# Graph layer on one Trainium2 core: the clique rows of the mix as two scaled f16 planes instead of three bf16 planes

## What is computed

```python
gathered = x_clique[clique_idx]                                   # edges x 128
summed = jax.ops.segment_sum(gathered, node_idx, num_segments=n_nodes)
count = jax.ops.segment_sum(jnp.ones(...), node_idx, num_segments=n_nodes)
mean = summed / jnp.maximum(count, 1.0)[:, None]
out = mean @ W.T + b
```

## Time and profile before

| what | value |
|---|---|
| median of 3 runs | 2649.56 us (2644.44 to 2656.32) |
| the profiled execution: its own time | 2649.81 us |
| its span | 2648.0 us |
| mean granted TensorE clock | 0.92 of full |
| PE busy | 2353.2 us, 89% |
| PEld busy | 2075.0 us, 78% |
| DVE busy | 1588.0 us, 60% |
| ACT busy | 1271.9 us, 48% |
| POOL busy | 109.5 us, 4% |

### The profile page before, as it was taken

How to read it: one execution, slowest core, us unless ns; L and a number is a source line. 1 busy time by engine, 2 the same in 40 slices (tenths; PEclk the granted TensorE clock), 3 DMA queues, 4 the chain that set the end, 5 groups by cost and what they waited for, 6 DMA issues and landing times.

```text
span 2648.0 us, 58999 instructions
## 1 busy us (share of the span) xinstructions
PE 2353.2 (89%) x20705; PEld 2075.0 (78%) x20705; DVE 1588.0 (60%) x2721; ACT 1271.9 (48%) x3044; POOL 109.5 (4%) x88
## 2 busy tenths in 40 slices
PE   1479999999999999999987799999998625999897
PEld 1369999999999999999975577777787614888644
DVE  8668777777777777777755555555575483000033
ACT  1246666666666666666611466666786410000133
POOL 3100000000000000000000000000000240000000
PEclk6589999999999999999965899999999857999899
DMA  5401111111111111111143422222384146888321
GB/s 166 123 33 73 73 68 54 73 73 73 49 73 73 73 58 63 73 73 69 52 114 92 173 106 105 105 105 105 138 315 164 48 117 255 300 302 299 98 62 56
DMA packets 183684, 299.35 MB, mean 113 GB/s; under 512 B 13256, under 2 KB 136523, under 8 KB 183523
## 3 DMA queue, kind: packets, MB, share of 16 engines
q1 hardware_dynamic: 179488, 284.33, 30.9%
q0 software_dynamic: 4144, 14.34, 1.9%
HBM read 198.15 MB, written 100.49 MB: 113 GB/s over the span
## 4 chain that ended last, share of the span: by engine, by line
PE 80%; DVE 9%; issue 3%; DVEq 3%; DMA 3%; ACT 1%; POOLq 0%; SPq 0%; POOL 0%; ACTq 0%; PEldq 0%
PE ps L703 21%; PE ps L762 18%; PE ps L692 15%; PE ps L686 8%; PE ps L746 7%; PE ps L801 4%; PE ps L895 2%; PE ps L732 2%; DVE hT_s L1272 1%; DVE carry L1469 1%; DVE big L1198 1%; DMA hs<-node_rows 1%; PE ps L620 1%; PE ps L792 1%; DMA big<-edge_counts 1%
## 5 line engine op out<-in xcount | busy, mean ns | idle before, releaser
L703 PE MATMUL ps<-big,rows_area 128*128 128x128 f32 x4802 | 659.6, 278 | 0.0
L703 PEld LDWEIGHTS ps<-big,rows_area 128*128 128x128 f32 x4802 | 587.6, 191 | 0.1
L1001 ACT CAST edge_area<-ps 128x392 f16<-128x392 f32 x784 | 380.9, 486 | 410.8 <-PE ps L686 410.8
L762 PE MATMUL ps<-big,rows_area 128*128 128x256 f16 (+1 forms) x4900 | 543.6, 272 | 25.9 <-DMA big<-edge_counts 25.9
L692 PE MATMUL ps<-edge_area 128*128 128x196 f16 x4704 | 540.7, 249 | 0.0
L762 PEld LDWEIGHTS ps<-big,rows_area 128*128 128x128 f16 x4900 | 469.6, 98 | 79.4 <-DMA big<-edge_counts 26.1
L692 PEld LDWEIGHTS ps<-edge_area 128*128 128x128 f16 x4704 | 421.4, 97 | 0.3
L1007 ACT COPY big<-ps 128x392 f32<-128x392 f32 x784 | 381.7, 487 | 29.8 <-PE ps L692 1.3
L686 PE MATMUL ps<-edge_area 128*128 128x196 f16 x2352 | 335.1, 250 | 15.2 <-DVEq L1421 15.2
L1416 DVE TENSOR_TENSOR edge_area<-lo_pair,carry 128x768 f16<-128x768 f16 x392 | 218.7, 558 | 211.5 <-PE ps L692 166.3
L1417 DVE TENSOR_TENSOR edge_area<-cell_pair,carry 128x1176 f16<-128x1176 f16 x392 | 299.6, 764 | 0.0
(11 more groups left out here) (210 smaller groups left out, 1650.5 us busy)
## 6 DMA issues: line engine op xcount, KB each, us to landing
big<-edge_counts SPq DMA_DIRECT2D x336, 448.0 KB, 4.9
edge_counts<-edge_area SPq DMA_DIRECT2D x49, 1568.0 KB, 5.7
hs<-node_rows POOLq DMA_DIRECT2D x21, 448.0 KB, 4.5
edge_area<-in_x SPq DMA_DIRECT2D x14, 448.0 KB
x_stream<-edge_area SPq DMA_DIRECT2D x14, 448.0 KB, 4.0
node_rows<-edge_area SPq DMA_DIRECT2D x14, 448.0 KB
edge_area<-x_stream SPq DMA_DIRECT2D x14, 448.0 KB, 3.9
node_rows<-rows_area SPq DMA_DIRECT2D x7, 448.0 KB
```

The source lines that it names most:

```text
L703: last = mm(p_sum[par], h0[:, n, :], w32[:, par, n, :], start=(n == 0), stop=(n == NB - 1))
L762: last = mm(p_block[par][:, 0:width, :], planes[:, p, sh, :], piece[:, par, k, 0:width, j, :], start=(sh == 0 and p == 0), stop=(sh == NB ...
L1001: nc.scalar.copy(store_slot[:, par, :, cols], p_count[s % 2]).then_inc(sem("count_taken"), 1)
```

## The change

The clique rows are no longer split into three bf16 planes. For each clique row VectorE takes the largest absolute value, keeps the exponent of it (a power of two, `xc_unit`), and scales the row by its inverse; the scaled row goes into two f16 planes. The mix then has two planes, 8 matmuls for 12. The power of two is put back on the other side of the product: ScalarE's copy of the flipped counts becomes an activation with a per-partition scale, `xc_unit`, and writes bf16 instead of f16. That copy therefore waits for the split of its own block, once at k = 0 of each block.

```diff
-        xc_plane = take(2 * 2 * 3 * D // 2, BF16).rearrange("p (s c l n) -> p s c l n", s=2, c=2, l=3)
+        xc_plane = take(2 * 2 * 2 * D // 2, F16).rearrange("p (s c l n) -> p s c l n", s=2, c=2, l=2)
         xc_in = take(2 * D)
-        xc_r = take(2 * D)
-        xc_r2 = take(2 * D)
-        flipped = take(4 * W // 2, F16).rearrange("p (s c n) -> p s c n", s=2, c=2)
+        xc_top, xc_inv = take(2), take(2)
+        xc_unit = take(4).rearrange("p (s c) -> p s c", s=2)
+        flipped = take(4 * W // 2, BF16).rearrange("p (s c n) -> p s c n", s=2, c=2)
...
-                            for l in range(3):
+                            for l in range(2):
                                 last = mm(p_mix[:, lo:hi], xc_plane[:, par, c, l, :], flipped[:, odd, c, lo:hi],
-                                          start=(c == 0 and l == 0), stop=(c == 1 and l == 2))
+                                          start=(c == 0 and l == 0), stop=(c == 1 and l == 1))
...
-                def copy_flip(n, c, odd):
+                def copy_flip(n, c, odd, par):
                     act.wait_ge(sem("flips"), n * 2 + c + 1)
                     act.sem_inc(sem("act_passed"), 1)
                     if c == 0:
 
                         act.wait_ge(sem("mixed"), n + 1)
-                    nc.scalar.copy(flipped[:, odd, c, :], p_flip[c]).then_inc(sem("flip_copied"), 1)
+                    nc.scalar.activation(flipped[:, odd, c, :], p_flip[c], ACT.Copy, scale=xc_unit[:, par, c:c + 1]).then_inc(
+                        sem("flip_copied"), 1)
...
                         if cliques:
-                            copy_flip(b * SUBS + k, 0, (par + k) % 2)
-                            copy_flip(b * SUBS + k, 1, (par + k) % 2)
+                            if k == 0:
+                                act.wait_ge(sem("xc_split"), b + 2)
+                                act.sem_inc(sem("act_passed"), 1)
+                            copy_flip(b * SUBS + k, 0, (par + k) % 2, par)
+                            copy_flip(b * SUBS + k, 1, (par + k) % 2, par)
...
-                rows, r, r2 = (v.rearrange("p (c d) -> p c d", c=2) for v in (xc_in, xc_r, xc_r2))
-                plane = [xc_plane[:, par, :, l, :] for l in range(3)]
+                rows = xc_in.rearrange("p (c d) -> p c d", c=2)
+                unit = xc_unit[:, par, :]
                 dve.wait_ge(sem("xc_loaded"), b * 16 + 16)
-                V.tensor_copy(plane[0], rows)
-                dve.drain()
-                V.tensor_tensor(r, rows, plane[0], ALU.subtract)
-                dve.drain()
-                V.tensor_copy(plane[1], r)
-                dve.drain()
-                V.tensor_tensor(r2, r, plane[1], ALU.subtract)
-                dve.drain()
-                V.tensor_copy(plane[2], r2).then_inc(sem("xc_split"), 1)
+                V.tensor_reduce(xc_top, rows, AX_X, ALU.max, apply_absolute_value=True)
+                dve.drain()
+                V.tensor_scalar(xc_top, xc_top, 1e-30, None, ALU.max)
+                dve.drain()
+                V.tensor_scalar(unit.bitcast(I32), xc_top.bitcast(I32), 0x7f800000, None, ALU.bitwise_and)
+                dve.drain()
+                V.reciprocal(xc_inv, unit)
+                dve.drain()
+                for c in range(2):
+                    V.tensor_scalar(xc_plane[:, par, c, 0, :], rows[:, c, :], xc_inv[:, c:c + 1], None, ALU.mult)
+                dve.drain()
+                for c in range(2):
+                    last = V.scalar_tensor_tensor(out=xc_plane[:, par, c, 1, :], in0=rows[:, c, :], scalar=xc_inv[:, c:c + 1],
+                                                  in1=xc_plane[:, par, c, 0, :], op0=ALU.mult, op1=ALU.subtract)
+                last.then_inc(sem("xc_split"), 1)
```

## The result

| | before | after |
|---|---|---|
| median of 7 runs each | 2653.03 us (2644.44 to 2658.07) | 2665.96 us (2661.53 to 2672.02) |
| the profiled execution, its own time (span) | 2649.81 us (2648.0) | 2672.02 us (2670.3) |
| mean granted clock | 0.92 | 0.90 |
| PE busy | 2353.2 us, 89% | 2322.1 us, 87% |
| first to last flip (line 732) | 1471.9 to 1891.9, 420.0 us | 1478.5 to 1910.9, 432.4 us |

A forecast was written before the change was run, and what follows sets the result against it. On averages PE alone set the pace, but the new wait would make it stand and lose its clock: +0.3 first block, +16.5 eleven more, +1.5 and -5.2 last, +13 on 2649.8 us, 2663 us; range 2632 to 2688.

The forecast's parts named there:

- Removed: In the mix, 4 of 12 matmuls go, 0.75 us less, so a step of PE becomes 3.83 us.
- The scaled copy: On ScalarE, the per-partition scale adds 0.2 us to a pair of copies, 1.9 us in light steps.
- The split: On VectorE, the new split of the clique rows takes 2.5 us, where the old takes 2.02.
- Flip 4 to copy 4: Within a block, from PE's flip 4 to ScalarE's copy of it: 0.90 us.
- Two heavy steps: ScalarE's steps with copies and a count, 4.98 us each, from copy 4 at 13.9 to copy 6 at 23.9.
- Count to split: At a block's end, from the start of ScalarE's last count to the split's start: 4.24 or 4.45 us.
- PE stands: Before flip 1, PE waits 4.6 us for ScalarE's first copy, once a block.
- The ring without the clock: From a block's first copy through PE, ScalarE's counts and VectorE's split to the next first copy: 32.75 us.
- The clock: After each PE wait, half rate for some 4 us delays flip 2, and so the block, by 1.5 us.
- The sum: Over the clique blocks: first block +0.3, eleven more +16.5, last block +1.5 and -5.2, together +13 us.
- Rival 1: PE waits before flip 1 as forecast but restarts at full rate: 2645 us, chance 0.15.
- Rival 2: VectorE's split is not late, so ScalarE's first copy directly follows its last count: 2602 us, chance 0.12.

The follow-up runs named there:

- filled wait: The changed kernel with 56 unread matmuls a block put into PE's idle time ahead of flip 1: 2642.0 us, ratio to before 0.9962.
- early split: The changed kernel with the split of the next block's clique rows moved to VectorE's step 4 of the block before: 2602.0 us, ratio to before 0.9812.
- two planes alone: The kernel before with the third plane left out of the mix, plain copies and no new wait: 2612.2 us, ratio to before 0.9845.
- longer split: The changed kernel with the first reduction of each split done three times instead of once: 2673.2 us, ratio to before 1.0077.
- interleaved counts alone: The changed kernel with counts dealt in turn to VectorE and ScalarE, the split left at its block's start: 2619.7 us, ratio to before 0.9888.
- the kernel with both: The changed kernel with the split moved into the block before (k = 5) and counts dealt in turn: 2585.3 us, ratio to before 0.9742.
- wait alone: The kernel before with only ScalarE's first copy of a block made to wait for that block's split: 2665.3 us, ratio to before 1.0047.

## Why the prediction was right

The forecast was 2663 us, slower or at the edge of it; measured were 2666.0, ratio 1.0057. Step by step, against the block from 1614.79 to 1648.83:

- Removed: PE's step 3.83 us, measured 3.82 (1621.86 to 1625.68). Right. The Trainium skill (TensorE: Matmul & The Clock Gate, "Back-to-back issue gap") has the 131 ns a matmul of 512 columns by which the forecast had its smaller alternative, 48 us. The trace does not agree: four matmuls fewer, two of 512 and two of 384 columns, made the step 0.76 us shorter, 190 ns each.
- The scaled copy: a pair 1.9 us, measured 1.90 to 1.91 (line 1046 has a mean of 1003 ns for 909). The Trainium skill (ScalarE: Activation LUTs, "What ACT_TABLE_LOAD costs") gives about 93 ns for each such operand; 94 here.
- The split: 2.5 us, measured 2.4. The three small operations took 0.17 each (0.16 taken), the reduction 0.41 (0.42), the pairs of 128x128 0.48 and 0.61 (0.61 each taken).
- Flip 4 to copy 4: 0.90, measured 0.74 (1629.50 to 1630.24). The 0.90 had been counted from the flip's weight load (1620.30), not from its first matmul (1620.46). Two heavy steps 9.96: copy 4 at 1630.24, copy 6 at 1640.20, 9.96. The split's end to the copy 0.2: 0.34.
- Count to split 4.35: 1641.99 to 1646.08, 4.09. The forecast took 4.24 and 4.45 from rows of before, where the end of a block stood behind VectorE's add of mix 5 and not behind the counts (in the block at 1599.78 the add ran to 1602.91, the last count was done at 1602.68). So that term was read from the wrong one of the two waits, 0.26 us too long.
- PE stands 4.6 us: 3.7 to 4.2 measured, since the ring is shorter than forecast. This was the least exact term; little hung on it, as the clock fell all the same.
- The ring without the clock 32.75 us: 32.3 with the wait filled. Most of the difference are the two terms that were too long (4.35 and the 0.90 from flip 4 to its copy).
- The clock 1.5 us a block: 1.7, by the filled wait. The two errors partly cancel: 34.25 us a block forecast, 34.0 measured. The forecast let the clock fall from the restart on; in half of the blocks it fell up to 1.5 us later, and cost 1.6 us there against 1.9 in the others.
- The sum: first block +0.3, eleven blocks +16.5, last block -3.7, together 13. Read from flip 1 to flip 1 they were -0.1, +14.4 and, up to the first product behind the clique blocks, -3.3: 11.0 us in the stage. By the medians it is 12.9, with an interval from 11 to 20. So the mechanism and each size were about right, and that the total agrees to 0.1 us is luck.
- Rival 1 (the clock stays, 2645) is what the filled wait makes of the kernel, 2642. Rival 2 (2602 us, if the split is not late) is what the early split measured, 2602. It had been priced without VectorE's own lateness, which the moved split removes too; with the split left in place, two planes alone show that lateness at 1.7 us a block.

Of the parts, on the kernel before: two planes -41 us, the wait +12.5, the scale nothing that can be told. Their sum is -28 and the change +13: the parts don't add, since the wait's price depends on PE's pace. With three planes PE stands 1.2 us and keeps its clock; with two it comes 3 us earlier to a release that is no earlier, stands 3.9 us and loses its clock. That last part is 1.7 us a block, some 20 us, by the filled wait. The new split by itself, 0.4 us longer than the old one, was not run alone; by the longer split each us in it is one us in the ring.

## What to carry to other kernels

When a change hands an engine a new input, ask where in the producer's queue the input is made and what that queue has just waited for; if it waited for the consumer, the two form a ring, whose length is worked out like a path and compared with the pace of the engine that bounds the kernel now. Here the input could be made half a block earlier, in an idle part of the producer's queue, and the same work went from 0.6% slower to 1.9% faster. An uneven load on an engine that is far from full can still bound a kernel: with the early split ScalarE was busy 75% of the time (253.5 of 340 us), and dealing its three heavy steps out between light ones gave a further 0.7%. And a chain read before a change need not be the one behind it: here VectorE's end of a block waited for PE's mix before and for ScalarE's counts after.

## What the runs showed of the hardware that I had not expected

Matmuls that compute nothing, put into a wait of 3.9 us, made the kernel 24 us faster, since they kept the granted clock at 1.00.

The length of a wait did not by itself decide whether the clock fell. From the rows of before I had a wait of 1.83 us without a fall and one of 2.86 us with one. In the kernel with interleaved counts alone a wait of 2.23 us (2.24 in one block) was followed by 1.2 GHz for over 3 us in three blocks and by no fall in three others, and one of 1.96 us (restart at 1508.94) was followed by a fall. Against that, a wait of 2.86 us in the early split (restart at 2031.54) and one of 3.35 us in the kernel with both (restart at 2029.84) left the granted clock at 1.00 in the stretches behind them, to 2040 us and to 2035 us (there PE stood again from 2031.7). In the clique stage the waits of up to 1.3 us (wait alone), 1.8 us (two planes alone) and 1.0 us (early split) were never followed by a fall.
